# Folding the setup stage into the front: input first, diagonals written by transfers

## What is computed

```python
x = x + mamba(layernorm(x))        # first layer
x = x + moe(layernorm(x))          # second layer

def mamba(x):                      # D_INNER = 1024, 16 states, 4 taps
    xn = (x - mu) * rsqrt(var + 1e-5) * ln_gamma + ln_beta
    x_ssm, z = split(xn @ W_in.T)
    x_ssm = silu(causal_conv(x_ssm, conv_w) + conv_b)
    xp = x_ssm @ W_xproj.T;  B, C = xp[1:17], xp[17:33]
    dt = softplus(xp @ W_dt.T + b_dt) + 0.001;  A = -exp(A_log)
    # for each step t:
    dA = exp(A * dt);  dB = (1 - dA) / (A + 1e-8) * B
    h = clip(dA * h + dB * x_t, -10, 10)
    y_t = sum(C * h) + D * x_t
    return (y * silu(z)) @ W_out.T

def moe(x):                        # weights of the top 2 of 7 gates, one expert matrix
    return x @ W_shared.T + sum(top2 weights) * (x @ W_expert.T) + bias
```

## Time and profile before

| | us |
|---|---|
| median of 3 runs | 4454.98 |
| lowest, highest | 4453.03, 4458.05 |
| profiled execution | 4454.84 |
| its span | 4453.1 |

### The profile page before, as it was taken

The page is one execution under the profiler, slowest core; times in us unless marked ns, Lnnn a source line. Parts: engine busy times, 40 slices in busy tenths (PEclk is TensorE's granted clock), DMA queues, the critical chain, the costliest instruction groups (busy, mean ns, idle before and its releaser), DMA issues. The chain is left out here.

```text
span 4453.1 us, 48998 instructions
## 1 busy us (share of the span) xinstructions
PE 4166.3 (94%) x14186; PEld 2461.5 (55%) x14186; DVE 3676.1 (83%) x4321; ACT 3171.4 (71%) x5821; POOL 3138.2 (70%) x1550
## 2 busy tenths in 40 slices
PE   2999999995999999999999999999999759999999
PEld 1777777774444444444444444444444238888887
DVE  5888888884899999999999999999999744444443
ACT  1666666664899999999999999999999611211111
POOL 0111111110899999999999999999999767777772
PEclk9999999997999999999999999999999879999999
DMA  5566566666576576656665766576656445555550
GB/s 187 190 203 207 186 208 212 214 205 196 152 191 189 155 184 185 184 155 186 187 181 156 193 186 172 158 197 188 168 168 181 142 157 162 169 163 175 176 166 30
DMA packets 581176, 786.71 MB, mean 177 GB/s; under 512 B 102800, under 2 KB 305936, under 8 KB 579368
## 3 DMA queue, kind: packets, MB, share of 16 engines
q1 hardware_dynamic: 570344, 762.57, 58.4%
q10 hardware_dynamic: 10560, 20.97, 1.3%
HBM read 540.17 MB, written 245.18 MB: 176 GB/s over the span
## 5 line engine op out<-in xcount | busy, mean ns | idle before, releaser
L965 POOL TENSOR_TENSOR q<-g,cc 128x1024 f32<-128x1024 f32 x1024 | 2394.6, 2371 | 139.7 <-DVE g L1105 120.6
L1105 DVE TENSOR_TENSOR_SCAN g<-dd,carry,ps_a 128x512 f32<-128x512 f32 x2048 | 2400.3, 1253 | 40.2 <-ACT ps_a L987 24.5
L1045 PE MATMUL ps_y<-q,w_s 128*128 128x512 f32 x4096 | 2098.4, 593 | 24.4 <-POOL q L965 12.7
L987 ACT ACTIVATE ps_a<-dt_s,small 128x512 f32<-128x512 f32 x2048 | 1501.7, 733 | 5.4 <-DVE g L1105 5.4
L976 ACT ACTIVATE dd<-ps_d 128x512 f32<-128x512 f32 x2048 | 1287.7, 629 | 74.7 <-PE ps_d L1032 51.7
L1032 PE MATMUL ps_d<-dm,xk 99*128 99x512 f32 x2048 | 1119.1, 547 | 63.7 <-ACT dd L976 25.9
L1032 PEld LDWEIGHTS ps_d<-dm,xk 99*128 99x128 f32 x2048 | 384.0, 188 | 1223.0 <-ACT dd L976 957.7
L1045 PEld LDWEIGHTS ps_y<-q,w_s 128*128 128x128 f32 x4096 | 778.6, 191 | 184.7 <-issue 59.3
L353 POOL TENSOR_TENSOR xnt_lo<-xnt_f,xnt_hi 128x512 fp32r<-128x512 f32 x64 | 112.5, 1758 | 557.1 <-ACT xnt_hi L378 557.1
L499 PE MATMUL ps_r_f<-xnt_hi,w_hi 128*128 128x512 f32 x1024 | 418.5, 409 | 13.8 <-DVE w_lo L672 13.8
L499 PE MATMUL ps_r_f<-xnt_lo,w_hi 128*128 128x512 f32 x1024 | 402.9, 393 | 0.0
(11 more groups left out here) (162 smaller groups left out, 4439.5 us busy)
## 6 DMA issues: line engine op xcount, KB each, us to landing
w_s<-w_d SPq DMA_DIRECT2D x256, 512.0 KB, 3.8
xk<-xt_d SPq DMA_DIRECT2D x768, 132.0 KB
xt_d<-xt_f SPq DMA_DIRECT2D x256, 256.0 KB, 3.1
cc<-c_d SPq DMA_DIRECT2D x128, 512.0 KB, 11.3
dm<-band_d SPq DMA_DIRECT2D x192, 264.0 KB
xs_d<-xs_f SPq DMA_DIRECT2D x128, 256.0 KB, 2.5
zs_d<-zs_f SPq DMA_DIRECT2D x128, 256.0 KB, 3.0
dt_d<-lg_f SPq DMA_DIRECT2D x32, 1024.0 KB, 6.5
```

Of the source, the lines that this page charges most:

```text
L965: pool.tensor_tensor(q[:, s % QB:s % QB + 2, :], g[:, s % GB:s % GB + 2, :], rows, ALU.mult).then_inc(s_q, 2)
L987: act.activation(ps_a[:, s % AB, :], dt[:, blk % DTB, :], ACT.Exp, scale=small[:, blk % MD, S_A + n:S_A + n + 1]).then_inc(s_a, 1)
L1045: pe.matmul(ps_y[:, blk % 2, :], w[:, half % WB, at:at + P], q[:, s % QB, :], start=(n == 0), stop=(n == NS - 1)).then_inc(s_n, 1)
L1105: dve.tensor_tensor_scan(g[:, s % GB, :], dd[:, m % 2, n, :], ps_a[:, s % AB, :], carry[:, m, n:n + 1], ALU.add, ALU.mult).then_inc(s_g, 1)
```

## The change

- The setup stage is gone; `front` takes over what it did. `load_x(0)` is the first transfer; `A_log`, `ln_gamma`, `ln_beta` follow, then `W_in` in four quarters of 1 MB, each with its own semaphore, then the small tensors. ACT and DVE make the upper and lower halves by quarters (`upper_win`, `lower_win`), ACT between the scalings of x; `project` waits for quarter q of the lower half only before it uses it (first chunk). PE no longer waits for the small loads before it transposes x.
- `-ea`, the limits, `inv` and `margin` are made by DVE after the halves; `small` stays in SBUF for the whole program instead of passing through `w_d`. PE transposes `inv` in chunk 0 (`turn_inverse`), DVE copies it, SP stores it to a new tensor `invt_d`: three copies and a block of zeros, 64 rows.
- No diagonal tile is built. SP writes zeros to `w_d` in chunks 0 to 7 (`clear_diagonal`, two halves of 0.5 MB per m, pieces of 512 B) and, a chunk later, the diagonals themselves from `inv` (`fill_diagonal`: 2,048 single elements). In chunks 8 to 11 it clears `band_d` (`clear_band`, 528 B pieces), in chunk 12 it fills the band of chunk 0. The first rows are cleared by `clear_edges` after `load_x(1)`.
- The gathers of `ba_d` are issued at the front's end and waited for there.
- The scan starts with `load_x(0, 0)`, without `fill_band(0)`, `small` and the gathers.
- In `ffn` the inverse is one load of 64 rows from `invt_d`, issued at once; the B and C rows are one load each with a leading dimension of four copies; POOL clears rows 64 to 127 of `inv` and `b_r` by copies.
- In the first chunk `xnt` alternates with a tile of `conv`; later `xnt` is one buffer, so that a scaling waits for POOL's use of the one before it.

```diff
@@ front, SP
                 load_x(0)
-                for stage, at in ((v, 0), (lg, KD // 2)):
-                    sp.dma_start(stage[:, :, :].rearrange("p m t -> p (m t)").rearrange("p (k n) -> p k n", n=2 * DI),
-                                 t_in["W_inT"][at * P:(at + KD // 2) * P, :].rearrange("(k p) n -> p k n", p=P))\
-                        .then_inc(s_wt, 16)
+                for dst, src in ((a_log, t_in["A_log"].rearrange("(m p) n -> p m n", p=P)),
+                                 (gamma[:, :], t_in["ln_gamma"]), (beta[:, :], t_in["ln_beta"])):
+                    sp.dma_start(dst, src).then_inc(s_gb, 16)
+                for k in range(KD):
+                    sp.dma_start(raw_win[k], t_in["W_inT"][k * P:(k + 1) * P, :]).then_inc(s_wq[k], 16)
...
+                load_x(1)
+                sp.wait_ge(s_pool, 1)
+                clear_edges()
+                sp.wait_ge(s_lo, KD + 1)
                 sp.dma_start(w_dt[2 * NX:NX3, :].bitcast(F32), low_dt.bitcast(F32)).then_inc(s_wt, 16)
-                load_x(1)
...
                     store_b(ch)
+                    if 0 < ch <= MD:
+                        sp.wait_ge(s_zero, 16 * (EDGES + 2 * ch))
+                        fill_diagonal(ch - 1)
+                    if ch < MD:
+                        clear_diagonal(ch, 0)
+                    elif ch < MD + 4:
+                        clear_band(ch - MD)
+                    elif ch == MD + 4:
+                        sp.wait_ge(s_bto, 32)
+                        sp.wait_ge(s_zero, 16 * (EDGES + 2 * MD + 8))
+                        fill_first_band()
                     store_zs(ch, 6)
                     store_turned(ch, 6)
                     load_x(ch + 2)
                     store_zs(ch, 7)
                     store_turned(ch, 7)
+                    if ch < MD:
+                        clear_diagonal(ch, 1)
                 for h in range(2):
                     store_dt(CHUNKS - 1, h)
                 sp.wait_ge(s_xpo, CHUNKS * 32)
+                for b in range(BATCH):
+                    gather_ahead(b)
+                sp.wait_ge(s_diag, 16 * (4 + MD + 2 + BATCH))
                 sp.wait_ge(s_dto, CHUNKS * 32)
...
+                def clear_diagonal(m, h):
+                    sp.dma_start(w_d[m, :, bass.ts(h, NS * P // 2)].rearrange("p (n k) -> p n k", k=P),
+                                 bcast(zeros[:, 0:1], [(0, NS // 2), (1, P)])).then_inc(s_zero, 16)
+                def fill_diagonal(m):
+                    whole = w_d[m, :, :]
+                    sp.dma_start(bass.AP(tensor=whole.tensor, offset=whole.offset, ap=[(W_PITCH + 1, P), (P, NS)]), inv[:, m, :],
+                                 allow_slow_non_contiguous=True).then_inc(s_diag, 16)
@@ front, ACT
-                act.wait_ge(s_wt, 13 * 16)
-                for q in range(KD):
-                    scale_xnt(0, q)
-                for j, stage in enumerate((v, lg)):
-                    act.activation(w_hi[:, 2 * j:2 * j + 2, :].rearrange("p k n -> p (k n)"),
-                                   stage[:, :, :].rearrange("p m t -> p (m t)"), ACT.Copy).then_inc(s_hi, 1)
+                act.wait_ge(s_gb, 48)
+                act.activation(ea, a_log, ACT.Exp).then_inc(s_ea, 1)
+                upper_win(0)
+                scale_xnt(0, 0)
+                scale_xnt(0, 1)
+                upper_win(1)
+                scale_xnt(0, 2)
+                scale_xnt(0, 3)
+                upper_win(2)
+                upper_win(3)
+                act.wait_ge(s_wt, 9 * 16)
                 act.activation(w_dt[:, :], raw_dt, ACT.Copy).then_inc(s_hi, 1)
@@ front, PE
-                pe.wait_ge(s_wt, 13 * 16)
+                pe.wait_ge(s_pool, 6)
                 for q in range(KD):
                     transpose_xn(0, q)
-                pe.wait_ge(s_lo, 2)
                 for ch in range(CHUNKS):
                     for m in range(MD):
                         project(ch, "x", m)
+                        if ch == 0 and m == 3:
+                            turn_inverse()
@@ scan, SP
-                fill_band(0)
-                sp.dma_start(small[:, :, :], w_d[:, :, W_BIG:W_COLS].rearrange("m p s -> p m s"),
-                             allow_slow_non_contiguous=True).then_inc(s_sm, 16)
                 load_x(0, 0)
-                sp.wait_ge(s_band, 32)
...
-                for b in range(BATCH):
-                    gather_ahead(b)
-                sp.wait_ge(s_ba, 16 * BATCH)
                 load_ahead(0)
@@ ffn, SP
-                            for r in range(3):
-                                at = dst[GROUP * r:GROUP * r + NS, :]
-                                sp.dma_start(at.bitcast(F32) if dst is b_r else at, src).then_inc(s_rows, 16)
+                            sp.dma_start(dst, bass.AP(tensor=src.tensor, offset=src.offset,
+                                                      ap=[(0, 4), (PAD, NS), (1, CH)])).then_inc(s_rows, 16)
...
-                sp.wait_ge(s_set, 3)
-                for r in range(3):
-                    for h in range(2):
-                        sp.dma_start(raw_inv[h][GROUP * r:GROUP * r + NS, :, :], w_d[h::2, 0:NS, W_INVT:W_INVT + P].rearrange("m n p -> n m p")).then_inc(s_wt[0], 16)
+                sp.dma_start(raw_inv, invt_d).then_inc(s_wt[0], 16)
                 load_rows(0)
```

More of the change, by code:

```diff
@@ L176, in front @@
-def front(nc, sb, sem, t_in, ident, ones, minus_half, margin, within, clips, xs_d, dt_d, zs_d, xp_d, xt_d, bt_d, c_d):
+            front(nc, sb, sem, t_in, ident, ones, minus_half, margin, within, clips, small, xs_d, dt_d, zs_d, xp_d, xt_d, bt_d, c_d,
+                  band_d, w_d, invt_d, ba_d)
+        scan(nc, sb, sem, clips, small, xs_d, dt_d, xt_d, bt_d, band_d, c_d, w_d, y_d, ba_d)
+        ffn(nc, sb, sem, t_in, ident, minus_half, xs_d, zs_d, xp_d, invt_d, y_d, out)
+def front(nc, sb, sem, t_in, ident, ones, minus_half, margin, within, clips, small, xs_d, dt_d, zs_d, xp_d, xt_d, bt_d, c_d,
+          band_d, w_d, invt_d, ba_d):
@@ L217, in front @@
         S = lambda n: sem("f_" + n, c)
-        s_wt, s_x, s_one, s_hi, s_lo, s_b1 = S("weights"), S("x"), S("one"), S("hi"), S("lo"), S("b1")
+        s_wt, s_x, s_one, s_hi, s_lo = S("weights"), S("x"), S("one"), S("hi"), S("lo")
+        s_wq = [S(f"wq{k}") for k in range(KD)]
+        s_gb, s_pool, s_ea, s_set = S("gb"), S("pool"), S("ea"), S("set")
+        s_ivm, s_ivt, s_zero, s_diag = S("ivm"), S("ivt"), S("zero"), S("diag")
         s_st, s_pow, s_xn, s_tr, s_te, s_xl = S("stats"), S("pow"), S("xn"), S("tr"), S("te"), S("xl")
@@ L742, in _, with scan @@
                 dve.wait_ge(s_fl, 3)
-def scan(nc, sb, sem, ident, clips, xs_d, dt_d, xp_d, xt_d, bt_d, band_d, c_d, w_d, y_d, ba_d):
+def scan(nc, sb, sem, clips, small, xs_d, dt_d, xt_d, bt_d, band_d, c_d, w_d, y_d, ba_d):
     STEPS = MD * NS
@@ L778, in scan @@
         S = lambda n: sem("s_" + n, c)
-        s_sm, s_band, s_ba = S("small"), S("band"), S("ba")
+        s_band, s_ba = S("band"), S("ba")
         s_dm = [S(f"dm{i}") for i in range(PIECES)]
@@ L1360, in upper_weights @@
                     act.activation(parts[i][1], parts[i][0], ACT.Copy).then_inc(s_hi, 1)
-                def upper_inverse():
-                    act.wait_ge(s_wt[0], 96)
-                    for h in range(2):
-                        last = act.activation(inv[:, h::2, :], raw_inv[h], ACT.Copy)
-                    last.then_inc(s_hi, 1)
                 def upper_y(ch):
```

289 lines of the change are left out of this document (130 added, 159 removed).

## The result

The changed kernel takes 4493.05 us (median of 4 runs, 4479.13 to 4503.94) against 4454.0 us before (4452.55 to 4458.05): a ratio of 1.008, 95% interval 1.007 to 1.0096. It is slower by 0.8%, where 4386.4 us was forecast. Its runs lie over 25 us, those of before over 5.5. The profiled execution took 4479.13 us, its span being 4476.9; it is the fastest of the four, so what follows, which is read from it, is kind to the change.

The account below looks back on a forecast made before the run. The prediction took PE to bound the front and POOL the scan, with savings at the opening and joints. Its terms, -64.4 + 8 + 3.5 - 3 - 10 - 2.5 = -68.4 us, took 4454.84 to 4386.4 us; range 4371 to 4406.

Parts of the forecast that it names:

- The opening: Start of the front: x load and first product come earlier as no setup stage stands before them; net -64.4 us.
- Rival (b): Opening: weight quarters land together near 18 us instead of 10, all that follows 6 us later; 4392; chance 0.12.
- Transfers in the chunks: Front's chunks: clearings, fills and bands issued ahead of the x load make it land later; +8 us, bounds 0 to +25.
- rival (a): Front's chunks: x is late, clearings at half rate hold the issuing queue; +25 for +8, about 4403; chance 0.13.
- End of the front and start of the scan: Joint: waiting for the gathers at the front's end +3.5 us, an earlier first product in the scan -3.
- The exposed gather: End of the front: gathers of `ba_d` are now waited for there; +3.5 us, bounds 0.5 and +9.5.
- The removed wait for the gathers: Start of the scan: `cc` loads no longer stand behind that wait; -10 us, bounds -6 and -12.3.
- The scan in its steady state: Scan after its start: POOL goes on at its pace; no term given.
- Start of the last stage: Last stage: fewer loads let SP issue the first `y_c` load sooner; -2.5 us, bounds 0 and -6.
- Rival (d): Front: slower than before, scattered fills of some 11 us each stall PE; at 13 us a fill about 4471; chance 0.03.

Follow-up runs that it names:

- both: The changed kernel with 32 bytes of padding in front and scan, and with fills and clearings issued behind the x load; 4387.6 us (0.9848).
- a_behind: The changed kernel with each chunk's fill, first clearing and band clearing issued behind the x load and last stores; 4440.62 us (0.9958).
- a_shift: The changed kernel with 32 bytes of padding ahead of the later tiles of front and scan; 4444.46 us (0.9968).
- best: `both` with gathers ahead of the last two dt stores, `dt_s` and `x_prev` moved, last-stage rows loaded four times 16 partitions; 4380.36 us (0.9829).
- best3: `best` with small tiles behind large ones and 64 bytes of padding, in scan and last stage only; 4370.2 us (0.9804).
- a_end: The changed kernel with all clearings, bands and fills together at the front's end, behind the last dt store; 4547.08 us (1.0198).
- both_fill: `both` with only the fill of a diagonal issued again ahead of the x load; 4395.03 us (0.9863).
- b_cc: The kernel before with `cc` of the scan moved by 32 bytes and a second pad behind it; 4501.56 us (1.0105).
- b_64: The kernel before with 64 bytes of padding ahead of `cc` in the scan; 4496.53 us (1.0087).
- b_shift: The kernel before with 32 bytes of padding in front and scan, nothing else changed; 4514.6 us (1.0122).

## Why the prediction was wrong

Against the forecast's own sum the profiled run is 92.2 us too long: 45 in the front, 40 in the scan, 4.6 in the last stage, 3.1 in the joint, less 0.4 in the opening.

Two steps failed and made the loss: the price of the transfers ahead of the x load (+8 forecast, +53.0 measured), and the scan's steady state, put at nothing (the whole scan -10 forecast, +29.9 measured). A third, the sign of the last stage's start, is small (-2.5, +2.1).

*The opening* was right, term by term: -64.8 for -64.4. Rival (b) is out: ACT started on the first quarter of the weights at 9.92 us.

*Transfers in the chunks*: the mechanism was right (x lands late, DVE waits beyond its cushions), the size wrong: +53.0 for +8, twice rival (a)'s +25. Two prices failed. Half a clearing was costed by the earlier trace rows, loads of large pieces at 380 GB/s; writes of 512 B pieces to DRAM ran at 152, 3.4 us for 1.4 (my upper bound was 2.6; half of 380 GB/s gives 2.8). The fill was costed by the earlier trace rows: 0.75 us at a share of 0.69 was turned into 0.5 us of sixteen full engines. But the elapsed time is 0.75 us, and the trace has 1,128 packets in it, so 2,048 pieces take 1.4 us even at that pace, and they took 2.1 to 2.5. Together 5.5 to 5.9 us stood ahead of x where I had 2.0 after deducting idle time. Beyond the cushions of 2.1 that is, as an estimate from these prices, about 3.6 us in each of eight chunks and 3 in the four with a band, some 40. The remaining 10 or so I put down to chunks that never caught up, as each x is issued from a queue that is already late; no run shows it. That the second halves cost nothing is borne out: in `both` all of it behind the x load costs 1.5 us over before, which is within what unchanged fronts differ by.

*The same term had a cure in it that I didn't weigh*: the order within the queue. On average over the front the DMA engines had room (share 0.61 before, 0.69 after); what stood ahead of x mattered.

*End of the front and start of the scan*: +3.6 for +0.5, but about 3 of this is the address effect: the joint is 75.2 us in the change and 75.4 in `a_behind`, 72.3 in `a_shift` and 72.0 in `both`. Without it the joint is +0.4 to +0.7. The exposed gather, which I set at +3.5 between 0.5 and 9.5, is at most 5.0 by `best` and 3.4 by `best3`. The section of the Trainium skill from which the prediction took its 2 us (DMA: Bandwidth & Descriptors, Anatomy of one DMA) describes transfers issued by GpSimd, and these are issued by SP; the queue's wait for them was 2.0 us in the change. The first product comes 2.5 us sooner after the queue's start, forecast 3. The removed wait for the gathers gave what was forecast: the scan from POOL's first `q` is 9.6 us shorter in `both`, forecast 10.

*The scan in its steady state* was costed at nothing, since the diff issues the same transfers there. It was 29.9 us longer in the profiled execution, where -10 from its start was forecast; `a_behind` and `a_end`, with the same tiles in the same places, have 2463.3 and 2459.6 us, so the 40 us are rather too few for the typical run. This is the only step that no rival had, and with the one before it it turned the sign. Either alone would have left a gain: with the x loads as late as they were, the kernel is 13 us faster than before once the tiles are moved back (`a_shift`, 4444.46 for 4457.29), and with the tiles badly placed but the order mended it is 17 us faster (`a_behind`, 4440.62). The profile of before could not show it. The diff did: `small` moved ahead of the scan's tiles.

*Start of the last stage*: +2.1 for -2.5. The earlier issue of `y_c` was right (6.0 us against POOL's last `q`), what it is worth wrong: the DMA engines were full there in both kernels (share 1.05 and 1.03), and the single transfers with four copies made the first tile late by 2.5 us. The rule of the Trainium skill (DMA: Bandwidth & Descriptors, Rules for kernel authors) on the leading dimension, weighed in the prediction, pointed this way; with it I had the term at about -1, still short of +2.1.

With both causes taken out, `both` has 4387.6 us, where 4386.4 was forecast. That agreement is partly luck: +8 in the chunks was 1.5 with the new order, -2.5 in the last stage was +2.3.

Rival (d), slower through the fills, named the right kind of object at the wrong price: it wanted 11 us a fill; they took 2.1 to 2.5, and `both_fill` shows 6.6 us in all. Rival (a) had the mechanism of the front at half its size. The other half of the loss, the places of the scan's tiles, none of the rivals had.

## What to carry to other kernels

Price a transfer by a row with the same direction and the same piece size, and by elapsed time, not by its busy share: 512 B pieces written to DRAM ran at 152 GB/s, where large loads had 380. In a queue that issues in order, put background transfers right behind the load that somebody waits for, not ahead of it: with clearings and fills ahead of it the front was 50 us longer, with all of them behind it 1.5 to 3.3. When a diff adds, drops or reorders allocations, look at where the tiles land that transfers write; keep their starts at multiples of 256 bytes and the small tiles behind them, and give a one-pad copy of the old kernel a run before looking for a cause in the change.

## What the runs showed of the hardware that I had not expected

- A start off 256 bytes of the scan's `cc`, `dm` and `xk`, which transfers write, costs that stage 17 to 59 us of 2,418 (0.7 to 2.4%), with 3 to 7% more DMA time per byte. The widest scatters (14 to 25 us, in `b_cc`, `b_64`, `b_shift` and the change) all belong to badly placed kernels, though other badly placed ones scattered by only 3 to 12; in the well placed ones it was 4 to 14.
- The same tiles' neighbours `w_s` and `dt_s`, also written by transfers, could be moved to multiples of 256 without any gain.
- PE at the full clock did 1.1% more matmuls in 500 us (2,302 for 2,276) when the last stage's large tiles started at multiples of 256; only the products of `y_hi` and `y_lo`, moved from 224 to 0, got shorter (395 to 390 ns), not those of tiles moved from 192 to 0.
- 4-byte pieces written to DRAM took 2.1 to 2.5 us for 2,048, at a DMA share of 1.7 and 3 GB/s.
